# Feed-forward computed on rows sorted by expert, and the queries of later batches computed beside the attention

## The reference

```
x += latent attention over ctx, masked by token ids  (16 heads, first 128 keys)
h  = layernorm(x)
shared = (silu(h @ shared_gate) * (h @ shared_up)) @ shared_down
top_val, top_idx = top_k(h @ router_w, 2)            # 2 of 8 experts
p = sigmoid(top_val)                                 # 0 for the other six
for e in 8 experts:  gate, up = split((p_e * h) @ gate_up_w[e])
                     out_e = (silu(gate) * up) @ down_w[e]
x += shared + sum_e out_e
x += quantised attention: q = qdq(layernorm(x)) @ qdq(wq).T + bq,
     16 heads of 16 columns over 1601 keys, qdq(o) @ qdq(wp).T + bp
x += relu(h @ W_up.T) @ W_down.T + (sum of two softmax weights) * (h @ W_expert)
```

## Time and profile before

| | us |
|---|---|
| median of three runs (lowest, highest) | 831.65 (827.65, 835.86) |
| the profiled execution, its time | 830.02 |
| the profiled execution, its span | 828.2 |
| TensorE matmul busy | 763.1 (92%) |
| VectorE busy | 578.5 (70%) |
| ScalarE busy | 383.8 (46%) |
| GpSimd busy | 187.4 (23%) |
| mean granted TensorE clock | 0.973 |

### The profile page before, as it was taken

One profiled execution on the slowest core, in us unless ns is written; L12 is line 12 of the kernel. 1 busy time (PEld: TensorE's weight loads), 2 busy tenths in 40 slices (PEclk: granted clock), 3 DMA queues, 4 the chain that ended last, 5 costly groups with the idle time before them and its releaser, 6 DMA issues.

```text
span 828.2 us, 13022 instructions
## 1 busy us (share of the span) xinstructions
PE 763.1 (92%) x5027; PEld 430.6 (52%) x5027; DVE 578.5 (70%) x1290; ACT 383.8 (46%) x563; POOL 187.4 (23%) x136
## 2 busy tenths in 40 slices
PE   7998999986999989889999899999899999899996
PEld 3533777763655655654444355554455554345434
DVE  3799776651656576597788777767687777897814
ACT  2100444342433323226666656556466566564680
POOL 2277432330640131120310403100405001300000
PEclk8799999999999999999999999999799999999999
DMA  9200200005199540345073390640580820550000
GB/s 307 115 0 0 81 0 2 1 0 182 54 121 156 117 49 20 48 58 87 1 133 47 135 126 1 134 59 1 162 98 14 144 36 1 115 65 7 9 1 13
DMA packets 32475, 55.93 MB, mean 68 GB/s; under 512 B 11572, under 2 KB 20532, under 8 KB 31509
## 3 DMA queue, kind: packets, MB, share of 16 engines
q1 hardware_dynamic: 32408, 55.04, 33.0%
HBM read 42.56 MB, written 12.46 MB: 66 GB/s over the span
## 4 chain that ended last, share of the span: by engine, by line
PE 63%; issue 15%; DVE 14%; POOL 6%; ACT 2%; DMA 1%; SPq 0%; POOLq 0%; DVEq 0%; ACTq 0%
PE ps L967 11%; PE ps L1078 10%; PE ps L1057 8%; PE ps L855 5%; DVE small L1637 4%; PE ps L865 3%; PE ps L787 3%; PE ps L824 3%; PE ps L931 3%; PE ps L911 3%; PE ps L814 2%; POOL r L614 2%; PE ps L743 2%; PE ps L803 1%; PE ps L1039 1%
## 5 line engine op out<-in xcount | busy, mean ns | idle before, releaser
L1637 DVE TENSOR_REDUCE small<-ps 128x1 f32<-128x400 f32 (+1 forms) x512 | 286.0, 573 | 86.4 <-PE ps L967 80.6
L1448 ACT ACTIVATE r<-ps 128x1024 f32<-128x1024 f32 (+1 forms) x208 | 212.4, 1023 | 91.6 <-PE ps L1057 88.7
L967 PE MATMUL ps<-r 96*128 96x400 bf16 (+1 forms) x512 | 172.3, 344 | 14.4 <-DVE small L1637 11.4
L1078 PE MATMUL ps<-r 128*17 128x256 f32 (+1 forms) x1664 | 132.0, 390 | 2.2 <-ACT r L1448 2.0
L1057 PE MATMUL ps<-r 99*128 99x256 bf16 (+1 forms) x832 | 127.5, 276 | 0.0
L967 PEld LDWEIGHTS ps<-r 96*128 96x128 bf16 x512 | 49.8, 97 | 128.2 <-DVE small L1637 93.8
L1057 PEld LDWEIGHTS ps<-r 99*128 99x128 bf16 (+1 forms) x832 | 82.3, 100 | 32.3 <-issue 10.0
L632 POOL TENSOR_TENSOR r<-r 128x1601 bf16<-128x1601 f32 x8 | 26.0, 3255 | 205.1 <-ACT r L1289 205.1
L911 PE MATMUL ps<-r,hT 128*128 128x512 f32 (+1 forms) x160 | 67.6, 554 | 1.0 <-DVE r L1626 1.0
L855 PE MATMUL ps<-r,wkvT 128*128 128x400 f32 (+1 forms) x128 | 53.4, 516 | 6.0 <-issue 6.0
L865 PE MATMUL ps<-wkvT,r 128*128 128x256 f32 (+1 forms) x208 | 57.0, 392 | 0.0
(11 more groups left out here) (201 smaller groups left out, 1036.9 us busy)
## 6 DMA issues: line engine op xcount, KB each, us to landing
r<-kscr SPq DMA_DIRECT2D x96, 200.1 KB, 8.7
kscr<-r SPq DMA_DIRECT2D x24, 400.2 KB, 4.1
r<-in_ctx_dram SPq DMA_DIRECT2D x4, 1601.0 KB, 7.3
r<-qscr SPq DMA_DIRECT2D x24, 128.0 KB, 5.2
r<-in_wo_dram SPq DMA_DIRECT2D x1, 2048.0 KB, 11.7
r<-in_gu_dram SPq DMA_DIRECT2D x1, 2048.0 KB, 7.7
qscr<-qpart SPq DMA_DIRECT2D x24, 64.0 KB, 1.7
x<-in_x_dram SPq DMA_DIRECT2D x1, 1024.0 KB, 5.3
```

What stands on the lines that cost most here:

```text
L967: mm(bank(ca % 2)[:, 0:m], qst[0:SROWS, h, q0:q0 + P], kst[0:SROWS, s % 2, h % HALF, a:a + m], start=True, stop=True).then_inc(mx_mm, 1)
L1078: last = mm(bank(6)[32 * k:32 * k + VW, 0:LQ], vx[0:n, b % 2, kt, h, :], pr[i % 3][0:n, k * LQ:(k + 1) * LQ], start=kt == 0, stop=kt == KT ...
L1448: fn(pr[i % 3][0:n, :], bank(2 + 2 * (i % 2), 2)[0:n, :], ACT.Exp, scale=SCALE1)\
L1637: v.tensor_reduce(mxc[quad % 2][:, n:n + 1], bank(ca % 2)[:, 0:m], AX_X, ALU.max).then_inc(mx_rdy, 1)
```

## The change

The feed-forward no longer computes all experts for all tokens. Each token's two choices become two copies of its normalised row, scaled by its probabilities; the copies are written to device memory at places sorted by expert, each expert's rows padded to whole tiles of 128. Which tile belongs to which expert is known only at run time, so the number of tiles is the worst case, and the expert of each tile is a register that selects the weights. The eight token tiles are treated in two groups: tiles 0 and 1 (at most 2*2+7 = 11 sorted tiles) and tiles 2 to 7 (2*6+7 = 19), 30 in all, taken in 15 pairs. The result rows are written to device memory and gathered back, two per token, and added (`join`). The shared expert stays dense, as four pairs of token tiles.

TensorE, the loop over the 19 items:

```
+            for n in range(FSTEPS):
+                if n < NI:
+                    gate_up(n)
+                if n + 1 < NI and ITEMS[n + 1][0] == "x":
+                    turn_sorted(ITEMS[n + 1][1])
+                if 2 <= n < NI + 2:
+                    weigh_down(n - 2)
+                if 1 <= n <= NI:
+                    turn_hidden(n - 1)
+                beside_first(ASIDE.get(n, []))
```

```
+            def gate_up(n):
+                what, i = ITEMS[n]
+                if what == "x":
...
+                    owners[n] = [pe.value_load(owner_at[0:1, j:j + 1], min_val=0, max_val=(E - 1) * D)
+                                 for j in (2 * i, 2 * i + 1)]
+                    pe.wait_ge(xt_ev, i + 1)
...
+                if n >= 2:
+                    pe.wait_ge(hid_rdy, n - 1)
+                for t in range(2):
+                    for k in range(FC):
+                        if what == "x":
+                            last = mm(bank(2 + n % 2)[:, t * D:(t + 1) * D], xsT[:, t, k, :],
+                                      gu[:, k, bass.ds(owners[n][t], D)], start=k == 0, stop=k == FC - 1)
...
+            def turn_sorted(i):     # waits for the load, 4 transposes into bank 4
+            def turn_hidden(n):     # waits for hidden(n), 2 transposes into bank 5
+            def weigh_down(n):      # waits for expert_out(n - 1), 2 products of 256 columns into bank 6
```

```
+            rsqrt_group(0)
+            rsqrt_group(1)
             sigmoid_power(0)
+            send(0)                 # 4 indirect scatters of 128 rows of 1 KB
+            sigmoid_power(1)
+            send(1)                 # 12 indirect scatters
+            for b in range(2):
+                fetch(b)            # 4 indirect gathers
+                rsqrt_query(b)
+                split_queries(b)
+            fetch(2)
+            split_keys(2)
+            rsqrt_query(2)
+            split_queries(2)
+            fetch(3)
+            rsqrt_query(3)
+            split_queries(3)
```

`fetch(b)` waits for the stores of its group and for the join of batch b-1, whose buffers it overwrites. SyncE, beside the loop:

```
+            for j in range(XRING):
+                load_sorted(j)
...
+            for n in range(NI + 3):
+                if 3 <= n and ITEMS[n - 3][0] == "x":
+                    store_sorted(ITEMS[n - 3][1])
+                if n + 1 < NI and ITEMS[n + 1][0] == "x" and ITEMS[n + 1][1] + XRING < PAIRS:
+                    load_sorted(ITEMS[n + 1][1] + XRING)
+                if n == 3:
+                    write_keys(0)
+                elif n == 5:
+                    stack_quad(0)
+                elif n == 6:
+                    write_keys(1)
+                elif n == 9:
+                    stack_quad(1)
+                elif n == QFIRST[-1] + 2:
+                    write_queries(0)
+                    stack_queries(0)
```

More of the change, by code:

```diff
@@ L96, in schedule @@
             put(start + 4 * KT + at, "tail", b, part)
+    for b in range(1, B):
+        for at, part in QPARTS:
+            put(QSTEPS[b] + at, "query", b, part)
     for quad in range(1, QUADS):
@@ new lines, in _, with bank7 @@
+            first_keys(1, 0)
+            route(0)
+            first_keys(1, 1)
+            first_keys(1, 2)
+            for i in range(1, TILES // 2):
+                turn_pair(i)
+            first_keys(1, 3)
+            route(1)
+            rank(0)
+            for j in range(4):
+                first_values(j)
+            rank(1)
+            for j in range(4, NV):
+                first_values(j)
+            taken = [(v_ev, NV)]
+            def bank7(reader, value):
+                pe.wait_ge(*taken[0])
+                taken[0] = (reader, value)
@@ L1185, in beside @@
                         tail(*a, between)
+                    elif what == "query":
+                        query(*a)
             shift(0)
-            pe.wait_ge(v_ev, NV + 5)
-            values(1, 6, 4)
             for quad in range(QUADS + 2):
@@ L1398, in beside @@
+            for n in range(FSTEPS):
+                if n < NI:
+                    silu(n)
+                if n + 1 < NI and ITEMS[n + 1][0] == "x":
+                    turned_sorted(ITEMS[n + 1][1])
+                if 1 <= n <= NI:
+                    turned_hidden(n - 1)
+                for what, *a in ASIDE.get(n, []):
+                    if what == "query":
+                        query(*a)
+                    elif what == "v":
+                        values_copy(*a, 7)
             def beside(quad, kt):
@@ new lines, in _, with stats_of, moments_of @@
+            v.memset(memb, 0.0)
+            def stats_of(tiles):
+                for t in tiles:
+                    last = v.bn_stats(statsf[:, t, :], x[:, t, :])
+                link(last)
+            def moments_of(g):
+                a, z = GROUPS[g]
+                for t in range(a, z):
+                    last = v.bn_aggr(mvf[:, t, :], statsf[:, t, :])
+                link(last)
+                v.tensor_scalar(mvf[:, a:z, 1], mvf[:, a:z, 1], LN_EPS, None, ALU.add).then_inc(eps_rdy, 1)
@@ L1709, in out_norm @@
+            for n in range(FSTEPS):
+                if n < NI:
+                    hidden(n)
+                if 2 <= n < NI + 2:
+                    expert_out(n - 2)
+                for what, *a in ASIDE.get(n, []):
+                    if what == "query":
+                        query(*a, lambda: None)
+                    elif what == "split":
+                        split_first_keys(*a)
+                    elif what == "max":
+                        max_chunk(*a)
             def out_norm(quad):
```

968 lines of the change are left out of this document (550 added, 418 removed).

## The result

The changed kernel took 859.06 us (median), the kernel before 833.75 beside it: a ratio of 1.0318, 95% interval 1.0263 to 1.0372. A later measurement of the same kernel on another chip gave 1.0282 (1.0213 to 1.035). The forecast was 817 us, the range 799 to 848. The profiled execution took 860.26 us. Each kernel ran four times; both medians count a single much longer execution (1518.7 and 899.4 us), and the ratio is of the fast runs alone.

What follows compares the result with a forecast made beforehand. It took TensorE to bound the dense feed-forward, with both TensorE and VectorE nearly full in the first attention quads. First exponential 36.8 us earlier, attention 21.9 longer: -14.9 us on 830.0, 815.1 plus 1.6, 817 us; range 799 to 848.

Steps and rivals of the forecast that it cites:

- (c): Waits inside the expert loop: indirect transfers 1.26 us each, scatters hidden, 5 us lost at batch 0's join plus 1.
- (e): Attention: VectorE's added query work costs 15.9 us in quads 0 to 2, the step 28 join 6; +21.9 us together.
- (a): Ahead of the experts: transposes, router products and waits add 11.7 us; experts start at 235.2 instead of 223.5.
- (b): Expert loop: 3.6 us per sorted pair, 0.2 of it register loads; 65.5 us up to step 19.
- R1: Slower rival: indirect transfers cost GpSimd 2 to 3.2 us each, by themselves or VectorE's key splits; 860 us, chance 0.2.
- (d): Queries of batch 0: first maximum at about 314, not 307; 32 maxima take 19.5 us; first exponential at 339.2.
- The lower clock: Lower granted clock in the new gaps of TensorE, said to add 1 to 3 us.
- R3: Faster rival: VectorE's room in quads 0 to 3 takes the queries, batch 3's gather is quick; 799 us, chance 0.17.

Runs made afterwards that it cites:

- e3: Changed kernel without register loads, each tile taking the weights of a fixed expert; ratio 1.0357 to the kernel before.
- e13: The changed kernel as it is, measured again on another chip; ratio 1.0282 to the kernel before, 854.72 us.
- e1: Changed kernel with the key-stack transfers sent behind the stores that the join of batch 0 needs; ratio 1.0085 to the kernel before, 835.61 us.
- e4: Changed kernel with VectorE's query work of batches 1 to 3 done on 8 of 512 columns; ratio 1.0193 to the kernel before, 845.81 us.
- e12: Changed kernel with GpSimd splitting only 8 of 1601 key columns for quads 4 and 5; ratio 1.0216 to the kernel before.
- e2: Changed kernel with the gathers of batch 3 issued ahead of the query split of batch 2; ratio 1.0216 to the kernel before, 846.31 us.
- e15: e5 plus idle TensorE products: 26 in the wait for the query stack, one before each maximum from the 17th; ratio 0.9996, 833.16 us.
- e9: e5 plus queries of batches 2 and 3 started later and quad 0's maxima two steps later; ratio 0.9786 to the kernel before, 813.86 us.
- e5: Changed kernel with the order edits of e1 and e2 together; ratio 1.009 to the kernel before.
- e8: e5 with the 32 maxima of quad 0 started two steps later; ratio 0.9968 to the kernel before, 829.37 us.

## Why the prediction was wrong, by its own steps

Against the forecast for the profiled execution (815.1) the changed kernel's 860.3 is 45.2 us more: the expert loop 20.6 (92.1 for 71.5), first maxima to first exponential 7.4 (39.9 for 32.5), the attention 17.2 (37.3 and 1.8, for 21.9), 0.7 behind the last exponential, less 0.7 at the start. The two large terms are (c) and (e).

(a) **Right in the sum.** The experts start at 234.5; 235.2 was forecast, and the last values waited 3.3 us where it had 4. One term is written wrongly: the transposes are 16 and not 32, so 14 are new, and 14 x 0.133 gives the 2 us; 30 would give 4.

(b) **Right, and too high.** A pair takes 3.25 us, not 3.6, and e3 shows that the register loads add nothing. At 3.25 the 15 pairs would have taken 5 us less than forecast, which hid as much of what (c) missed.

(c) **This is the step that failed.** Not in the price of an indirect transfer: that was right to the hundredth, by luck, for the 1.26 us was the mean of a GpSimd subtraction that has nothing to do with a transfer. Two gathers in GpSimd's timeline of the changed kernel, 1.26 us apart:

```profile
442.05 0.96 POOL L796 DMA_INDIRECT hT<-yscr,pos  x1 [0.30 <-issue]
443.31 0.95 POOL L796 DMA_INDIRECT y<-yscr,pos  x1 [0.30 <-issue]
```

R1's price is false here: its time, 860, was met by another cause. What was missing is the wait for the ring, which the sum had at nothing. The sum followed one store behind `stack_quad(1)` and asked only when the join's data would land; it never asked who waits for the other stores' landing. With two buffers and six 200 KB transfers ahead, VectorE's copy waits, and TensorE behind it: 6.70 us here, 9.8 in e13, and slow products behind it. The gap behind the join, 6.08 us, was in the sum (6). Beside the ring stand the gap near 245 (3.74) and the low clock behind each of the three gaps (an estimate: half of the 13.6 us of products in the first three rows at 1.2 GHz below, 6.8). e1 shows the cause: 16 to 19 us came back from the order of SyncE's transfers alone.

(d) **Right in the wait, short behind it.** 7.6 us for the query stack (7 forecast). The 32 maxima then took 24 us instead of 19.5. Part of that is the clock: the first four stand 1.19 us apart, beside values' products of 1.06 us at 1.2 GHz that take 0.59 at 2.4. Another part is TensorE's wait for ScalarE's copy of the values, 0.52 us about once in four maxima.

(e) **Right in kind, short by 17.2 us.** Quads 0 to 2 were to take 31, 27.7 and 29.7 + 6 us; they took 33.7, 31.2 and 44.9. The added VectorE work was to cost 15.9 us. e4 takes nearly all of it away and 10 us come back, of which some 5.6 belong to one pass that GpSimd held up (e12), a term that the sum had at nothing. The gap at step 28 was foreseen with 6 us lost; TensorE stood for 10.53, behind VectorE's wait for the gathers of batch 3:

```profile
448.28 0.69 DVE L1925 TENSOR_TENSOR x<-x,hT 128x512 f32<-128x512 f32 x1 [9.62 <-DMA y<-yscr,pos]
450.24 0.52 PE L1218 MATMUL ps<-r 96*128 96x401 bf16 x1 [10.53 <-DVE small L1972]
```

Behind that gap the clock is 1.2 GHz until 456.4. e2, which moves these gathers alone, takes 7.2 us off quad 2.

The lower clock "would add 1 to 3 us". Windows of the seven stretches at 1.2 GHz between 240 and 460 us in the changed kernel:

```profile
248.20:251.60 3.40, 3.20 (x8) 2.58 (x9) 2.42 (x3) 0.34 (x2) 0.00 (x0) 0.50 0.29 77
272.10:278.90 6.80, 3.92 (x10) 3.18 (x11) 1.12 (x3) 0.38 (x1) 0.00 (x0) 0.50 0.89 322
302.80:313.10 10.30, 6.44 (x18) 4.69 (x19) 5.86 (x18) 1.85 (x4) 0.73 (x1) 0.50 0.26 78
333.60:340.40 6.80, 4.47 (x12) 3.28 (x13) 2.11 (x4) 0.60 (x1) 0.00 (x0) 0.50 0.38 82
360.90:371.10 10.20, 8.14 (x40) 3.52 (x44) 5.38 (x14) 4.96 (x5) 0.00 (x0) 0.50 0.81 136
415.50:422.30 6.80, 6.02 (x32) 2.27 (x33) 5.29 (x15) 2.05 (x2) 0.72 (x1) 0.50 0.67 221
442.80:456.40 13.60, 5.88 (x29) 1.83 (x29) 6.75 (x17) 1.22 (x2) 2.82 (x4) 0.50 0.73 112
```

TensorE is busy for 38 of these 57.9 us, and would need half of it at 2.4 GHz: an estimate of up to 19 us, if all of it were on the path. Each stretch stands behind a gap or a run of products with gaps between them. How much of the 19 is real stays open: e2 shows 3.6 us in one quad, e15 2.4 us in the first maxima, without a gain in the whole.

R3 was nearest where VectorE is concerned, and its 799 needed the waits to be absent. With four edits of order and no arithmetic altered (e9) the change does bring time, 814 us: most of what it lost lay in the order of queues and steps.

Not settled: the gap near 245. ScalarE stood for 5.3 to 6.3 us, in the last 3.7 to 4.4 of them with its product finished, in five profiles (the first of the changed kernel, and e5 to e8, which shared a chip), and in none of the twelve others of the changed kernel and its variants. No transfer of instructions stands in the DMA queues between 238 and 250 us there.

## What to carry to other kernels

When transfers are added to a queue that a prefetch already uses, follow every one of them to the buffer that its landing frees, and count how many steps the ring gives it: a bulk transfer whose own data is needed more than 60 us later can still hold up a short one that somebody waits for. Put two-input VectorE passes where GpSimd's long ones are not. And price a gap of the bounding engine at more than its length, since the products behind it can run at the lower clock; here taking the gap away paid, and filling it did not.

## What the hardware showed unexpectedly

An indirect transfer of 128 rows of 1 KB costs GpSimd mostly 0.96 us, 1.26 from one to the next, also beside VectorE's maxima. But one of the scatters took longer:

```profile
241.84 1.75 POOL L783 DMA_INDIRECT xscr<-r,pos  x1 [0.30 <-issue]
242.47 1.00 DVE L1916 CAST r<-r 128x1601 bf16<-128x1601 f32 x1
```

It ends 0.12 us behind the end of VectorE's conversion of 1601 columns; the transfer ahead of it, beside the first pass of the same key split alone, took 0.96. In the 17 traces of the changed kernel and its variants 34 of 544 indirect transfers took over 1.25 us (1.74 to 2.56), one to three in each, and all of them lie beside VectorE's key splits: 22 end 0.11 to 0.13 us behind that conversion, the other 12 lie beside the third pass. The prediction said that no run showed whether VectorE can hold up a transfer's issue; these speak for it, though no run takes the passes away. The waiting cost GpSimd 0.8 us in the first profile of the changed kernel and 4.1 in e13; what of that reached the time isn't shown, but the part of R1 that named the key splits was right in kind.

Two register loads per 3.25 us of products cost TensorE nothing. And where idle work held the clock up in one stretch (0.94 for 0.77), the clock of quads 2 and 3 was lower afterwards (0.86 and 0.81 for 0.88 and 0.89), in one profile of each.
